# Low part of the first expert's down weights in each ring of four: made one unit later on VectorE, beside that of the second expert

## The chip, the cores and the metric

The kernel runs on one core of a Trainium2 chip. The metric is device time in microseconds (us) of one execution; lower is better. All positions in the trace are us from the start of the profiled span.

## The reference

One perceiver layer on x of shape (2, 128, 256), in float32: cross attention to 2048 context tokens (16 query heads, 8 key heads), causal self attention, and then the part in which the change lies, a mixture of experts:

```
shared = silu(x @ shared_gate_w) * (x @ shared_up_w) @ shared_down_w
comb   = weights of the 2 best of 16 experts for each token
for e in range(16):
    g, u = split(x @ experts_gate_up[e])
    routed = routed + comb[:, e:e+1] * (silu(g) * u @ experts_down[e])
out = x + shared + routed
```

Each expert has gate and up weights of 256 x 256 and down weights of 128 x 256. There are 256 token rows.

## The kernel before

Matrix products are made from float32 data split in two: a "high" part (the value rounded to the TensorE format fp32r) and a "low" part (value minus high part). Each product is three matmuls: low with high, high with low, high with high (lines 586 to 588). So every weight needs a rounding and a subtraction before TensorE may use it.

The expert stage handles 17 experts, numbered m = 0 to 16; m = 0 is the shared one, m = 1 to 16 are the routed ones. Weights live in rings of four slots (slot s = m % 4), and the loops step over rings: m = 4 i + s. Every engine has its own queue of instructions in program order, and they meet at semaphores:

- SyncE (SP) loads weights. For expert m it waits until the gate-up low part of m - 4 is made (`gu_ready`), issues the gate-up load (line 418), waits until the down low part of m - 4 is made (`dn_ready`), and issues the down load (line 420). Experts 0 to 7 are loaded long before the stage; 8 to 16 are loaded inside it.
- ScalarE (ACT), in its unit m: `silu` of the gate half (line 1528), then `round_gu`, the rounding of the gate-up weights of m + 3 (line 1542), which waits for their load; then the rounding of the gated rows (line 1559), then `round_dn`, the rounding of the down weights of m + 1 (line 1548).
- GpSimd (POOL): the low part of the gate-up weights, once they are rounded (line 455, from line 550). It begins with expert 4, when the router on VectorE is through.
- VectorE (DVE), in its unit m: `gated`, gate times up (line 2009); `add_expert` of m - 3, two instructions that add the product of an earlier expert to the rows (line 2047; line 2058 for the shared one); `rest_h`, the low part of the gated rows (line 2014); and the low part of the down weights of m + 1 (line 2066).
- TensorE (PE): `gate_up(m)`, 12 matmuls, then `down(m - 2)`, 6 matmuls. gate_up(m) waits for gate-up weights and for `gated` of m - 2. down(m) waits for the low parts of its weights and rows, and in the loop for `added3`, which comes with `add_expert(m - 2)`, that is with the additions of VectorE's unit m + 1:

```
pe.wait_ge(dn_ready, m + 1)
pe.wait_ge(h_lo_ready, m + 1)
after(pe, added3, B * (m - (RING if isinstance(m, int) else 2) + 1))
```

The loads on SyncE, in the order in which they are issued:

```
sp.wait_ge(gu_ready, m - RING + 1)
sp.dma_start(ring_gu[:, s], exgu_v[m - 1]).then_inc(ld_gu[s], 16)
sp.wait_ge(dn_ready, m - RING + 1)
sp.dma_start(ring_dn[:, s, :], ex_down_w[m - 1]).then_inc(ld_dn[s], 16)
```

In ScalarE's unit:

```
round_gu(m + 3, t, ...)     # waits for ld_gu[t]
act.wait_ge(h_ready, m + 1)
act.activation(hT_hi[:, s], hT[:, s % 2], ACT.Copy).then_inc(h_hi_ready, 1)
```

Of the kernel before, what the change touches and what calls it, by code (L numbers as in the profile page):

```python
# [5 lines left out]
ALU = mybir.AluOpType  # L6
ACT = mybir.ActivationFunctionType
AX = mybir.AxisListType
F32 = mybir.dt.float32
# [21 lines left out]
def perceiver_layer(nc, x, ctx_tokens, key_mask, xq_w, xk_w, xv_w, xo_w, sq_w, skv_w, sd_w,  # L31
                    gate_w, expert_bias, sh_gate_w, sh_up_w, sh_down_w, ex_gu_w, ex_down_w, out):
    B, T, H = x.shape
    _, KEYS, VIS = ctx_tokens.shape
    assert B == 2 and T == P and VIS == P and H == 2 * P
    HB = H // P
# [10 lines left out]
    E = gate_w.shape[1]  # L47
    F = ex_down_w.shape[1]
    RING = 4
# [30 lines left out]
    with ExitStack() as stack:  # L80
# [3 lines left out]
        def sem(name):  # L84
            return stack.enter_context(nc.semaphore(name))
# [17 lines left out]
        with nc.sbuf_tensor("first_pT", [P, J, NBLK, P], F32) as first:  # L103
# [63 lines left out]
            for v in (ctx_hi, ctx_lo))  # L167
        dn_hi, dn_lo = (v[:].rearrange("p b i d -> p (b i d)")[:, RING * HB * 2 * F:][:, 0:RING * H]
                        .rearrange("p (s n) -> p s n", s=RING) for v in (ctx_hi, ctx_lo))
# [12 lines left out]
        ring_dn = ctx_raw[:, 2048:3072].rearrange("p (s n) -> p s n", s=RING)  # L182
# [34 lines left out]
        def turned_block(f, s):  # L217
# [56 lines left out]
        dn_hi_ready, dn_ready, h_hi_ready, h_lo_ready = (  # L274
            sem("dn_hi_ready"), sem("dn_ready"), sem("h_hi_ready"), sem("h_lo_ready"))
# [306 lines left out]
        def _(pe):  # L582
# [336 lines left out]
            def query(r, head, cols, done):  # L919

                dst, h = (QA, QB)[head // 2], head % 2
                _, hi, lo = wq2_of[r % 2]
                for k in range(HB):
                    at = (k * HR + head) * P
                    last = product(dst[:, h * B * T + cols.start:h * B * T + cols.stop],
                                   (hi[:, at:at + P], lo[:, at:at + P]),
                                   [v[:, cols] for v in XT[k]], k == 0, k == HB - 1)
                if h == 1:
                    last.then_inc(done, 1)
# [644 lines left out]
        def _(dve):  # L1574
# [432 lines left out]
            def gated(m, s):  # L2007
                dve.wait_ge(silu_ready, m + 1)
                dve.tensor_tensor(hT[:, s % 2], GU[s % 2][:, B * T:2 * B * T], sg[:, s % 2],
                                  ALU.mult).then_inc(h_ready, 1)  # L2010

            def rest_h(m, s):
                dve.wait_ge(h_hi_ready, m + 1)
                dve.tensor_tensor(hT_lo[:, s], hT[:, s % 2], hT_hi[:, s].bitcast(F32),
                                  ALU.subtract).then_inc(h_lo_ready, 1)
# [27 lines left out]
            def add_expert(m, s):  # L2043
                dve.wait_ge(down_psum, m + 1)
                for b in range(B):
                    dve.wait_ge(added3, B * (m - 1) + b + 1)
                    dve.scalar_tensor_tensor(resid[:, b, :], DWN[s][:, b * H:(b + 1) * H],  # L2047
                                             comb[:, b, bass.ds(m - 1, 1)], resid[:, b, :],
                                             ALU.mult, ALU.add).then_inc(added3, 1)

            def unit(i, s, dn_on):
                m = RING * i + s
                gated(m, s)
                if isinstance(m, int) and m == RING - 1:

                    dve.wait_ge(down_psum, 1)
                    rows = resid[:].rearrange("p b n -> p (b n)")
                    dve.tensor_tensor(rows, DWN[0][:], rows, ALU.add).then_inc(added3, B)
                elif not isinstance(m, int) or m >= RING:
                    add_expert(m - 3, (s - 3) % RING)  # L2060
                rest_h(m, s)
                if dn_on:

                    dve.wait_ge(dn_hi_ready, m + 2)
                    t = (s + 1) % RING
                    dve.tensor_tensor(dn_lo[:, t], ring_dn[:, t], dn_hi[:, t].bitcast(F32),
                                      ALU.subtract).then_inc(dn_ready, 1)

            router()

            dve.wait_ge(dn_ready, RING)
            for s in range(2, RING):
                unit(0, s, s == RING - 1)
            with dve.Fori(1, E // RING - 1) as i:
                for s in range(RING):
                    unit(i, s, True)
            for s in range(RING):
                unit(E // RING - 1, s, s < RING - 1)
            add_expert(E - 3, 1)
            gated(E, 0)  # L2080
            add_expert(E - 2, 2)
# [35 lines left out]
```

## Time and profile before

| | |
|---|---|
| median of 3 runs | 344.44 us (343.89 to 344.46) |
| profiled execution, its time | 343.99 us |
| its span, first to last instruction | 342.2 us |
| mean granted TensorE clock | 0.993 |
| expert stage | from about 299 us to 340 us |

The span is what the trace shows; the execution's time lies 1.8 us above it. In rows of the timeline the columns are start and length in us, engine, line, operation, output <- inputs, shapes, count, and in brackets the idle time before with what ended it. In this part of the kernel `ctx_raw` holds the weights as loaded, the gated rows and the silu; `ctx_hi` and `ctx_lo` hold the high and low parts of the weights; `pT_hi` and `pT` hold those of the gated rows; `pair` and `bank` are PSUM banks.

### The profile page before, as it was taken

To read this page: it belongs to the slowest core of one execution; us is meant where nothing else is said; L and a number is where in the kernel's file an instruction comes from. 1 tells how busy PE (TensorE), PEld (TensorE's weight loads), DVE (VectorE), ACT (ScalarE), POOL (GpSimd) and SP (SyncE) were. 2 spreads that over 40 slices of the span, in tenths; PEclk is the share of its full clock that TensorE was granted. 3 is DMA by queue.
4 is the path that set the end of the run, shared out by engine and by line. 5 is a ranking of instruction groups with operands and counts; after the bars stand their busy time and mean duration, and the time that the engine had idled before them with its cause. 6 is when DMAs were issued, how large, how long until landed. Compare 5 with 4: busy or idle time off the path is not lost.

```text
span 342.2 us, 6811 instructions
## 1 busy us (share of the span) xinstructions
PE 329.7 (96%) x2222; PEld 299.0 (87%) x2222; DVE 270.4 (79%) x466; ACT 229.2 (67%) x410; POOL 220.2 (64%) x136
## 2 busy tenths in 40 slices
PE   6999988999999999999999999999999999899995
PEld 5887867999999999999999989899898897699995
DVE  2776888898988989889889889676558736479997
ACT  3799449586688777777777675993256666267761
POOL 3766709799499599499588786853625873117550
PEclk9999999999999999999999999999999999989999
DMA  6811558875896895885875976995052045004530
GB/s 211 244 33 38 115 134 192 218 167 132 219 211 140 205 206 124 213 200 124 200 183 115 206 176 175 204 268 178 2 164 84 0 156 153 3 0 131 178 107 32
DMA packets 32565, 49.98 MB, mean 146 GB/s; under 512 B 5536, under 2 KB 23072, under 8 KB 32544
## 3 DMA queue, kind: packets, MB, share of 16 engines
q1 hardware_dynamic: 32544, 49.72, 57.4%
q8 instruction: 11, 0.18, 0.2%
q14 instruction: 10, 0.08, 0.1%
HBM read 20.08 MB, written 0.26 MB: 59 GB/s over the span
## 4 chain that ended last, share of the span: by engine, by line
PE 86%; DVE 6%; ACT 4%; issue 2%; POOL 1%; DVEq 0%; POOLq 0%; ACTq 0%
PE bank L586 12%; PE bank L587 12%; PE bank L588 12%; PE pair L586 11%; PE pair L588 11%; PE pair L587 11%; PE bank L984 2%; PE bank L790 2%; PE bank L1014 1%; ACT probs L1253 1%; PE pair L977 1%; PE bank L977 1%; ACT first_pT L1334 1%; PE pair L943 1%; DVE resid L2047 1%
## 5 line engine op out<-in xcount | busy, mean ns | idle before, releaser
L455 POOL TENSOR_TENSOR pT<-pT,pT_hi 128x1024 fp32r<-128x1024 f32 x54 | 129.3, 2418 | 34.5 <-ACT pT_hi L1263 34.4
L1253 ACT ACTIVATE probs<-probs,lowest 128x2048 f32<-128x2048 f32 x32 | 64.4, 2012 | 23.3 <-DVE lowest L1650 23.3
L1263 ACT ACTIVATE pT_hi<-pT 128x1024 fp32r<-128x1024 f32 x56 | 57.7, 1055 | 12.7 <-DMA pT<-ctx_raw 11.6
L587 PE MATMUL bank<-pT,ctx_hi 128*128 128x256 f32 x224 | 64.2, 287 | 0.0
L586 PE MATMUL bank<-pT_hi,ctx_lo 128*128 128x256 f32 x224 | 63.9, 285 | 0.0
L588 PE MATMUL bank<-pT_hi,ctx_hi 128*128 128x256 f32 x224 | 63.6, 284 | 0.0
L586 PE MATMUL pair<-ctxT_hi,qk_lo 128*128 128x512 f32 x128 | 52.2, 408 | 0.0
L588 PE MATMUL pair<-ctxT_hi,qk_hi 128*128 128x512 f32 x128 | 50.1, 391 | 0.0
L587 PE MATMUL pair<-ctxT_lo,qk_hi 128*128 128x512 f32 x128 | 50.0, 391 | 0.0
L1650 DVE CUSTOM_DVE_ANT_0 probs<-pair,mask_bias,lowest 128x1024 f32<-128x1024 f32 x32 | 40.9, 1280 | 10.2 <-PE pair L588 9.5
L455 POOL TENSOR_TENSOR ctx_lo<-ctx_raw,ctx_hi 128x512 fp32r<-128x512 f32 (+1 forms) x19 | 31.4, 1666 | 23.8 <-ACT ctx_hi L1542 17.5
L1650 DVE CUSTOM_DVE_ANT_0 probs<-pair,mask_bias 128x1024 f32<-128x1024 f32 x32 | 38.5, 1205 | 6.7 <-PE pair L588 3.8
L586 PEld LDWEIGHTS bank<-pT_hi,ctx_lo 128*128 128x128 f32 x224 | 42.3, 189 | 1.7 <-POOL pT L455 0.8
L587 PEld LDWEIGHTS bank<-pT,ctx_hi 128*128 128x128 f32 x224 | 42.1, 188 | 1.0
L588 PEld LDWEIGHTS bank<-pT_hi,ctx_hi 128*128 128x128 f32 x224 | 42.7, 191 | 0.0
L1661 DVE STREAM_TRANSPOSE ctx_raw<-probs 128x2048 f32<-128x2048 f32 x14 | 32.0, 2308 | 0.5 <-PE bank L790 0.5
L1661 DVE STREAM_TRANSPOSE blocks<-probs 128x2048 f32<-128x2048 f32 x14 | 31.9, 2306 | 0.0
L588 PEld LDWEIGHTS pair<-ctxT_hi,qk_hi 128*128 128x128 f32 x128 | 24.0, 188 | 5.4
L586 PEld LDWEIGHTS pair<-ctxT_hi,qk_lo 128*128 128x128 f32 x128 | 24.1, 188 | 3.2
L587 PEld LDWEIGHTS pair<-ctxT_lo,qk_hi 128*128 128x128 f32 x128 | 24.2, 189 | 3.1
L586 PE MATMUL pair<-xnT_hi,ctx_lo 128*128 128x256 f32 x64 | 18.4, 288 | 0.0
L587 PE MATMUL pair<-xnT_lo,ctx_hi 128*128 128x256 f32 x64 | 18.4, 288 | 0.0
(280 smaller groups left out, 794.3 us busy)
## 6 DMA issues: line engine op xcount, KB each, us to landing
pT<-blocks SPq DMA_DIRECT2D x112, 128.0 KB, 2.3
pT<-ctx_raw SPq DMA_DIRECT2D x112, 128.0 KB, 2.3
ctx_raw<-ffn_experts_gate_up_dram SPq DMA_DIRECT2D x16, 256.0 KB, 2.9
wq<-in_L_xattn_Wq_dram SPq DMA_DIRECT2D x8, 256.0 KB, 2.7
ctx_raw<-in_ctx_dram SPq DMA_DIRECT2D x8, 256.0 KB, 6.5
wo<-in_L_xattn_Wo_dram SPq DMA_DIRECT2D x8, 256.0 KB, 3.0
blocks<-in_L_attn_w_dense_dram SPq DMA_DIRECT2D x4, 512.0 KB, 4.8
ctx_raw<-_L_ffn_experts_down_dram SPq DMA_DIRECT2D x16, 128.0 KB, 2.4
```

The source lines that it names most:

```text
L455: pool.tensor_tensor(dst, src, hi.bitcast(F32), ALU.subtract).then_inc(ready, 1)
L586: pe.matmul(dst, w[1], x[0], start=start, stop=False)
L587: pe.matmul(dst, w[0], x[1], start=False, stop=False)
L588: return pe.matmul(dst, w[0], x[0], start=False, stop=stop)
L790: last = pe.matmul(dst, ctx_raw[:, blk * P:(blk + 1) * P], first_pT[:, :, blk, :], start=(blk == 0), stop=(blk == NBLK - 1))
L943: last = pe.matmul(KV[:, (B + b) * P:(B + b + 1) * P], xnT[:, k, b * T:(b + 1) * T], wv2[:, k], start=(k == 0), stop=(k == HB - 1))
L977: mm = pe.matmul(SC[b][:, h * P:(h + 1) * P], q2T[:, h, b * T:(b + 1) * T], k2T[:, b * T:(b + 1) * T], start=True, stop=True)
L984: pe.matmul(PC[b][:], v2[:, b], p2T[:, b], start=True, stop=True).then_inc(c2_psum, 1)
L1253: act.activation(probs[:, j], probs[:, j], ACT.Exp, bias=lowest[:, p, j, 1:2], scale=-1.0, accum_out=den[:, p, j:j + 1]).then_inc(exps, 1)
L1263: act.activation(hi_slot(c), chunk(p, c).bitcast(F32), ACT.Copy).then_inc(pT_hi_ready, 1)
L1650: dve.tensor_tensor_reduce(out=probs[:, j, keys], in0=pair[m % 2][:], in1=mask_bias[:, p, keys], scale=-SCALE, scalar=lowest[:, p, j, 0:1] ...
L1661: dve.transpose(blocks[p][:, :, j].rearrange("p q k t -> p k q t"), probs[:, j].rearrange("p (k q t) -> p k q t", q=QD, t=LN)).then_inc(tu ...
```

## The change

VectorE's unit (i, s) now makes the low part of the down weights of expert 4 i (slot 0) in unit s = 0 of the same ring, behind `rest_h`, and right behind it that of expert 4 i + 1; units s = 1 and 2 make that of m + 1 as before; unit s = 3 makes none. Before, slot 0 of the next ring was made in unit s = 3. The number of instructions is the same (12), and each waits for its own rounding.

```
+            def rest_dn(m, t):
+                dve.wait_ge(dn_hi_ready, m + 1)
+                dve.tensor_tensor(dn_lo[:, t], ring_dn[:, t], dn_hi[:, t].bitcast(F32),
+                                  ALU.subtract).then_inc(dn_ready, 1)
+
...
                 rest_h(m, s)
-                if dn_on:
-
-                    dve.wait_ge(dn_hi_ready, m + 2)
-                    t = (s + 1) % RING
-                    dve.tensor_tensor(dn_lo[:, t], ring_dn[:, t], dn_hi[:, t].bitcast(F32),
-                                      ALU.subtract).then_inc(dn_ready, 1)
+                if dn_on and s == 0:
+                    rest_dn(m, 0)
+                if dn_on and s < RING - 1:
+                    rest_dn(m + 1, s + 1)
 
             router()
 
             dve.wait_ge(dn_ready, RING)
             for s in range(2, RING):
-                unit(0, s, s == RING - 1)
+                unit(0, s, False)
             with dve.Fori(1, E // RING - 1) as i:
                 for s in range(RING):
                     unit(i, s, True)
             for s in range(RING):
-                unit(E // RING - 1, s, s < RING - 1)
+                unit(E // RING - 1, s, True)
```

## Rows read from the trace of the kernel before

**Rows 1.** The page, busy time of each engine and its share of the span.

```profile
PE 329.7 (96%) x2222; PEld 299.0 (87%) x2222; DVE 270.4 (79%) x466; ACT 229.2 (67%) x410; POOL 220.2 (64%) x136
```

**Rows 2.** Busy time by stretch, for 6 us inside the expert stage.

```profile
318.00:324.00 6.00, 6.00 (x52) 5.95 (x51) 6.00 (x15) 4.61 (x12) 3.66 (x3) 1.00 0.56 172
```

**Rows 3.** Timeline of PE: last matmul before down(3), its first, down(6)'s, down(10)'s.

```profile
311.56 0.28 PE L588 MATMUL pair<-xnT_hi,ctx_hi 128*128 128x256 f32 x1
312.23 0.39 PE L586 MATMUL bank<-ctx_hi,pT 128*128 128x256 f32 x1 [0.40 <-DVE resid L2047]
...
318.73 0.39 PE L586 MATMUL bank<-ctx_hi,pT 128*128 128x256 f32 x1
...
327.46 0.29 PE L586 MATMUL bank<-ctx_hi,pT 128*128 128x256 f32 x1
```

**Rows 4.** Timeline of DVE: end of unit 3, units 4 and 5; rest_h(7); gated(15).

```profile
309.53 1.52 DVE L2066 TENSOR_TENSOR ctx_lo<-ctx_raw,ctx_hi 128x256 fp32r<-128x256 f32 x1
310.98 0.41 DVE L2009 TENSOR_TENSOR ctx_raw<-pair,ctx_raw 128x256 f32<-128x256 f32 x1
311.31 0.86 DVE L2047 SCALAR_TENSOR_TENSOR resid<-bank,route,resid 128x256 f32<-128x256 f32 x2
312.10 0.41 DVE L2014 TENSOR_TENSOR pT<-ctx_raw,pT_hi 128x256 fp32r<-128x256 f32 x1
...
312.77 0.41 DVE L2009 TENSOR_TENSOR ctx_raw<-pair,ctx_raw 128x256 f32<-128x256 f32 x1
...
318.60 0.76 DVE L2014 TENSOR_TENSOR pT<-ctx_raw,pT_hi 128x256 fp32r<-128x256 f32 x1
...
334.70 0.42 DVE L2009 TENSOR_TENSOR ctx_raw<-pair,ctx_raw 128x256 f32<-128x256 f32 x1 [0.16 <-ACT ctx_raw L1528]
```

**Rows 5.** Timeline of POOL: gate-up low parts of experts 4 to 7, then of 10.

```profile
306.60 5.60 POOL L455 TENSOR_TENSOR ctx_lo<-ctx_raw,ctx_hi 128x512 fp32r<-128x512 f32 x4 [9.20 <-ACT ctx_hi L1542]
...
317.77 1.30 POOL L455 TENSOR_TENSOR ctx_lo<-ctx_raw,ctx_hi 128x512 fp32r<-128x512 f32 x1 [0.83 <-ACT ctx_hi L1542]
```

**Rows 6.** Waits of SP's queue: us in total, times, longest.

```profile
SPq L420 <- DVE ctx_lo L2066: 10.9, 9, 2.6
```

**Rows 7.** Timeline of SP: down 8 and gate-up 9, down 12 and gate-up 13.

```profile
311.21 0.35 SPq L420 DMA_DIRECT2D ctx_raw<-_L_ffn_experts_down_dram  x1
311.81 0.37 SPq L418 DMA_DIRECT2D ctx_raw<-ffn_experts_gate_up_dram  x1
...
319.85 0.34 SPq L420 DMA_DIRECT2D ctx_raw<-_L_ffn_experts_down_dram  x1
320.44 0.37 SPq L418 DMA_DIRECT2D ctx_raw<-ffn_experts_gate_up_dram  x1
```

**Rows 8.** From issue to landing, us: gate-up load 9; all nine; down loads too.

```profile
ctx_raw<-ffn_experts_gate_up_dram SPq DMA_DIRECT2D x1, 256.0 KB, 3.0
...
ctx_raw<-ffn_experts_gate_up_dram SPq DMA_DIRECT2D x9, 256.0 KB, 2.8
...
DMA to landing us min/median/max: 2.0/2.6/3.2
```

**Rows 9.** Timeline of ACT: silu(4), round_gu(9), round_gu(13), silu(15).

```profile
309.74 0.38 ACT L1528 ACTIVATE ctx_raw<-pair 128x256 f32<-128x256 f32 x1 [0.47 <-PE pair L588]
...
314.94 0.62 ACT L1542 ACTIVATE ctx_hi<-ctx_raw 128x512 fp32r<-128x512 f32 x1
...
323.58 0.62 ACT L1542 ACTIVATE ctx_hi<-ctx_raw 128x512 fp32r<-128x512 f32 x1
...
334.28 0.39 ACT L1528 ACTIVATE ctx_raw<-pair 128x256 f32<-128x256 f32 x1 [0.43 <-PE pair L588]
```

**Rows 10.** Busy time by stretch around the router: after PE, PEld, DVE, ACT, POOL, the granted clock.

```profile
297.00:298.00 1.00, 0.16 (x1) 0.14 (x1) 0.56 (x3) 0.00 (x1) 0.40 (x1) 1.00 0.00 0
...
300.00:301.00 1.00, 1.00 (x7) 1.00 (x6) 0.90 (x4) 1.00 (x1) 0.00 (x0) 0.50 0.00 0
...
303.00:304.00 1.00, 1.00 (x9) 1.00 (x8) 0.83 (x6) 0.18 (x2) 0.00 (x0) 0.82 0.00 0
```

## The prediction

> **What bounds the kernel now.** I read the page first: PE is busy 96% of the span [rows 1]. The change touches only the expert stage, so I then took the table by stretch there. In 6 us of it PE and DVE are both busy all the time, ACT 4.61 us, POOL 3.66 us, at full clock [rows 2]. Two engines at 100% call for the timelines, to see which waits for which. A unit on PE takes 2.13 us: 18 matmuls, about 0.118 us apart; 12 of gate_up take 1.42, 6 of down 0.71. PE really waits at one place: the last matmul of gate_up(5) starts at 311.56, so down(3) could start at 311.68, and it starts at 312.23, released by the additions on DVE (line 2047) [rows 3]. Those end at 311.31 + 0.86 = 312.17 [rows 4], so additions to PE takes 0.06. Its first matmul has 0.39 where others have 0.28: the load of its weights is no longer hidden behind matmuls, 0.1 more. down(6) shows the same 0.39 at 318.73, while down(10) at 327.46 has 0.29 [rows 3]. So PE sets the pace and DVE's additions come just in time, with 0 to 0.2 to spare.
>
> DVE's own work in a unit is less than 2.13: starts lie 0.33 apart for gated, 0.79 for two additions, 0.33 for rest_h, 0.33 for the down subtraction, 1.78 in all. The rest is a blockage. POOL works from 317.77 to 319.07 [rows 5]; rest_h(7) starts at 318.60 and takes 0.76 instead of 0.41 [rows 4], ending at 319.36, 0.29 behind POOL. The down subtraction in unit 3 takes 1.52 us and ends at 311.05, 0.25 behind the third of POOL's four in a row, of 1.4 each [rows 4, 5]. That instruction is the one that the change moves out, and it is what made down(3) late.
>
> Last, the waits of SP's queue: nine times line 420 waits for DVE line 2066, 10.9 us in total [rows 6]. Each down load waits for the very subtraction that is moved, and the gate-up load of the next expert stands behind it in the same queue.
>
> **The change, part by part.** It adds no work: 12 subtractions stay 12. Four effects follow.
>
> *Unit 3 loses its subtraction (gain).* Where DVE is free, gated starts 0.42 behind silu: 334.28 and 334.70 [rows 4, 9]. So gated(4) can start at 309.74 + 0.42 = 310.16, not 310.98. The additions end 0.33 + 0.86 later, at 311.35. down(3) starts at 311.68: 0.55 + 0.1 = 0.65 gained.
>
> *Unit 4 has two subtractions (loss).* rest_h(4) still ends behind POOL's fourth, which ends 306.60 + 5.60 = 312.20 [rows 5], perhaps 0.13 earlier as DVE no longer disturbs it: 312.35. Subtractions end at 312.68 (expert 4) and 313.01 (expert 5), gated(5) follows, and the additions end at 314.13. PE reaches down(4) at 311.68 + 0.71 + 1.42 = 313.81 and starts at 314.19 + 0.1, where before it started at 314.46. So 0.65 shrinks to about 0.2 within one unit. In the later rings the second subtraction alone would make the additions 0.33 later where they have 0.16 to spare: 0.17 + 0.06 + 0.1, some 0.3 a ring.
>
> *The loads.* Before, the subtraction of expert 4 ended at 311.05, down load 8 was issued at 311.21 and gate-up load 9 at 311.81, 0.60 behind [rows 4, 7]. Now it ends at 312.68, so down 8 goes out at 312.84 and gate-up 9 at 313.44. Its landing took 3.0, the nine have a median of 2.8 [rows 8]; I take 2.9: 316.35. Before, it landed at 314.81 and ACT used it at 314.94 [rows 9]: 0.13 to spare against 1.63 of delay. gate_up(6) now ends at 312.39 + 1.42 + 0.16 = 313.97, silu(6) follows at 314.12, and 0.28 later, at 314.40, ACT wants the load. It stands for 1.95.
>
> *What is queued behind that wait.* round_gu(9) then ends at 316.35 + 0.62 = 316.97. Behind it on ACT stands the rounding of gated rows 6, done at about 317.4; POOL starts 0.08 behind round_gu, at 317.05, and holds DVE's rest_h(6) until 318.35 + 0.28 = 318.63. The subtraction starts at 318.55, gated(7) at 318.88, the additions at 319.21, ending at 320.07. down(6), which needs them, starts at 320.13 instead of 318.73: **+1.4**. The gain of 0.2 is inside this number.
>
> Of these 1.4, POOL's hold on DVE is a good half: were rest_h(6) free at 317.4, it would end at 317.8 and down(6) would start near 319.3, +0.6. The Trainium skill's page SBUF — State Buffer, section "Who interferes with whom", says that a VectorE instruction with two SBUF inputs and a GpSimd instruction that reads SBUF exclude each other, and that whoever issued first keeps the port for its whole instruction. By that rule it is +1.4, and the 0.76 of [rows 4] agrees; without it, it would be +0.6.
>
> *The second ring.* PE now runs 1.4 late, so DVE and ACT have caught up with it, and the double subtraction costs nothing there: the rounding of gated rows 7, held up by gated(7), lets ACT come to silu(8) at 320.05 and round_gu(11) at 320.33, POOL's low part of 11 runs from 321.03 to 322.33, rest_h(8) ends at 322.61, the subtraction of expert 8 at 322.94. down 12 goes out at 323.10, gate-up 13 at 323.70 (before 320.44 [rows 7]), landing 2.8 later, 326.5. gate_up(10) ends at 324.66 (before 323.26), and ACT wants to round at 324.98 (before 323.58 [rows 9]). It stands for 1.5. The same chain follows: round 0.62, POOL to 328.5, rest_h(10) to 328.78, subtraction, gated, additions to 330.23, down(10) at 330.3 instead of 327.46 [rows 3]: **+2.8** in all.
>
> *The third ring.* There is no gate-up load 17, and down load 16 (out at about 333 now) lands 2 us later, with the last product wanted at 340. Gate-up 16 lands by 332.6, wanted at 333.0: 0.4 to spare. Small waits of PE such as that at 318.73, here some 0.1 in all, vanish as DVE now has slack. The tail is tied to PE and moves with it.
>
> Sum: 1.4 + 1.4 - 0.1 = +2.7. On the profiled execution's 343.99 that is 346.7; the median of the runs lies 0.45 above that execution, so 347.1 on it. I say 347.0.
>
> Bounds: all loads of the stage, the half as large down loads too, landed within 2.0 to 3.2 [rows 8], so each wait may be up to 0.8 shorter or 0.3 longer: +1.1 to +3.3. The gate-up loads are nearest to their own median of 2.8. Not shown in the trace is how ACT behaves when it waits for a load in this stage; from below it costs nothing beyond the landing, as I take it, from above 0.1 each.
> The Trainium skill's page DMA: Bandwidth & Descriptors, section "Anatomy of one DMA", fits a load as 2.0 us plus bytes over 436 GB/s (for loads issued by GpSimd); for 256 KB that is an estimate of 2.6 us. With it the sum would be about +2.2; the measured 2.8 to 3.0 decide.
>
> **The rivals.**
> *One stall only.* The delay that the first wait gives PE might serve the second ring as slack: if DVE, far ahead, gets rest_h(8) in before POOL's instruction at 321.03, expert 8's low part is done 1.6 earlier and gate-up 13 comes in time. For it: ACT starts silu(8) at once after the hold-up, and DVE adds are over at about 321.6, only 0.6 behind POOL's start. Against: 0.6 is more than what any small shift gives. +1.3: 345.3 to 345.8. Chance 0.10.
> *The clock falls.* Before, the granted clock was 1.00 while PE was busy 0.16 of a us at 297, and it stood at 0.50, the lower of its two levels (1.2 GHz), from 300 until within the us from 303 [rows 10], with PE busy throughout. The new waits leave PE idle for about 1.5 each. A low spell of some 3.2 us at half the clock does 1.6 us of full-clock work, so it loses 1.6. Behind the first wait it would be mostly absorbed by the second (PE wants gate-up 13 later too); behind the second it is paid: 2.7 + 1.6 = +4.3, 348.3 to 348.7. Against: both waits lie between dense stretches, and the shorter wait at 312 has full clock behind it [rows 2]. Chance 0.10.
> The Trainium skill's page TensorE: Matmul & The Clock Gate, section "The HAM clock gate", says that the low clock is the idle state and that sustained activity lifts it, which leaves this open.
> *The loads are hidden anyway*, because ACT's wait falls in time that nobody needs. Then the first ring gives 0.2, the others lose 0.3 each: +0.1 to +0.4, 344.1 to 344.8. Against: only 0.13 to spare [rows 8, 9]. Chance 0.06.
> *Faster.* The moved subtraction frees unit 3 from POOL's four in a row, and the 0.65 at down(3) stays gained, with the waits at down(6) and its like, 0.35 in all: -1.0, 343.0 to 343.4. It decides if rest_h(4) and both subtractions end before 312.0, so before POOL's fourth. That one starts at about 310.8, and rest_h(4) can't before 311.35. Chance 0.04.
>
> **How the numbers follow.** Forecast 0.70, with its own range of 345.9 to 347.7 (each wait 0.3 off, on either base). One stall 0.10, clock 0.10, hidden 0.06, faster 0.04. 345.3 to 348.7 leaves out hidden and faster, 1 in 10. A measurement of this kernel can tell 0.2%, 0.7 us, from no change: faster is 0.04, within is 0.07 (the hidden case and a little of the one-stall case), slower is 0.89.
>
> **What would show it.** In the profile of the changed kernel: down(3) starts without the 0.40 of idle time; gate-up load 9 is issued near 313.4 and 13 near 323.7; ACT line 1542 waits twice for a DMA, 1.5 to 2 us each; POOL and then rest_h (line 2014) follow, over 1 us long each time; PE waits twice for DVE line 2047, at down(6) and down(10), about 1.5 each; the third ring runs without waits. I am wrong if line 1542 has no wait for DMA, if PE's waits lie elsewhere, or if the clock is at 0.50 after them.

## The result and the profile after

The changed kernel takes 347.19 us (median of 4 runs, 347.02 to 347.58) against 344.29 us: ratio 1.0087, interval 1.0075 to 1.0100, so 2.9 us slower. The forecast was 347.0 with a range of 345.3 to 348.7. The profiled execution took 347.58 us, its span is 345.8 us, the mean granted clock 0.993 as before.

The table by stretch, for the same 6 us as [rows 2] (the columns are PE, PEld, DVE, ACT, POOL, then the clock). PE was busy all of them before; now it has 4.53:

```profile
318.00:324.00 6.00, 4.53 (x39) 4.33 (x38) 6.00 (x14) 4.09 (x11) 3.36 (x4) 1.00 0.41 116
```

The waits from 303 us on (us in total, times, longest):

```profile
ACT ctx_hi L1542 <- DMA ctx_raw<-ffn_experts_gate_up_dram: 4.2, 4, 2.0
...
PE bank L586 <- DVE resid L2047: 2.7, 2, 1.5
...
PE pair L586 <- DVE resid L2047: 0.2, 1, 0.2
```

The first line is new: ScalarE's rounding of gate-up weights waits for the loads, four times. PE waits for the additions twice in earnest. The timeline of PE, first matmuls of down(3), down(4), down(6) and down(10), to be held against [rows 3]:

```profile
312.07 0.28 PE L586 MATMUL bank<-ctx_hi,pT 128*128 128x256 f32 x1
...
314.55 0.39 PE L586 MATMUL pair<-ctx_hi,pT 128*128 128x256 f32 x1 [0.18 <-DVE resid L2047]
...
320.54 0.39 PE L586 MATMUL bank<-ctx_hi,pT 128*128 128x256 f32 x1 [1.47 <-DVE resid L2047]
...
330.62 0.39 PE L586 MATMUL bank<-ctx_hi,pT 128*128 128x256 f32 x1 [1.19 <-DVE resid L2047]
```

The wait at down(3) is gone, a smaller one has come at down(4), and then two long ones. Upstream of them, SP's queue (against [rows 7]), with down 8 and gate-up 9, down 12 and gate-up 13:

```profile
313.19 0.35 SPq L420 DMA_DIRECT2D ctx_raw<-_L_ffn_experts_down_dram  x1
313.79 0.37 SPq L418 DMA_DIRECT2D ctx_raw<-ffn_experts_gate_up_dram  x1
...
323.40 0.35 SPq L420 DMA_DIRECT2D ctx_raw<-_L_ffn_experts_down_dram  x1
324.00 0.37 SPq L418 DMA_DIRECT2D ctx_raw<-ffn_experts_gate_up_dram  x1
```

ACT's round_gu(9), round_gu(10) and round_gu(13) (against [rows 9]), each with the wait for its load:

```profile
316.75 0.63 ACT L1542 ACTIVATE ctx_hi<-ctx_raw 128x512 fp32r<-128x512 f32 x1 [1.97 <-DMA ctx_raw<-ffn_experts_gate_up_dram]
...
318.87 0.63 ACT L1542 ACTIVATE ctx_hi<-ctx_raw 128x512 fp32r<-128x512 f32 x1 [0.61 <-DMA ctx_raw<-ffn_experts_gate_up_dram]
...
326.84 0.63 ACT L1542 ACTIVATE ctx_hi<-ctx_raw 128x512 fp32r<-128x512 f32 x1 [1.35 <-DMA ctx_raw<-ffn_experts_gate_up_dram]
```

Loads 9 and 13 landed 2.9 and 2.8 us behind their issue. Load 10 stood in a row of six loads that SP issued 0.54 to 0.60 apart from 313.19 on; it went out at 314.89 and took 3.9 us, where before it took 3.2. ACT's waits for loads 10 and 14 are short (0.61 and 0.23 us), ACT waits for `gated` behind each of them anyway (0.23 and 0.60 us), and PE doesn't wait for them.

POOL follows each long wait, and holds DVE (against [rows 5, 4]). First POOL's gate-up low parts of 9 and 13:

```profile
317.46 1.29 POOL L455 TENSOR_TENSOR ctx_lo<-ctx_raw,ctx_hi 128x512 fp32r<-128x512 f32 x1 [2.91 <-ACT ctx_hi L1542]
...
327.55 1.29 POOL L455 TENSOR_TENSOR ctx_lo<-ctx_raw,ctx_hi 128x512 fp32r<-128x512 f32 x1 [2.30 <-ACT ctx_hi L1542]
```

Then DVE: gated(4), rest_h(4), the two subtractions of unit 4, and rest_h(6):

```profile
310.56 0.42 DVE L2009 TENSOR_TENSOR ctx_raw<-pair,ctx_raw 128x256 f32<-128x256 f32 x1 [0.56 <-ACT ctx_raw L1528]
...
311.70 1.00 DVE L2014 TENSOR_TENSOR pT<-ctx_raw,pT_hi 128x256 fp32r<-128x256 f32 x1
312.62 0.75 DVE L2053 TENSOR_TENSOR ctx_lo<-ctx_raw,ctx_hi 128x256 fp32r<-128x256 f32 x2
...
317.72 1.31 DVE L2014 TENSOR_TENSOR pT<-ctx_raw,pT_hi 128x256 fp32r<-128x256 f32 x1 [1.44 <-ACT pT_hi L1559]
```

rest_h(6) starts at 317.72, POOL has been at work since 317.46 and ends at 318.75, and rest_h(6) ends at 319.03, 0.28 behind it, for 1.31 us instead of 0.41. The third ring has no wait of PE over 0.1.

All of this lies in a profile that enters the stage 0.40 us later than the one before: down(2) starts at 309.94 instead of 309.54. To compare executions I use **the stage**: from the first matmul of down(2) to the first of down(14). Before it is 336.17 - 309.54 = 26.63, after it is 339.41 - 309.94 = 29.47: +2.84. The profiled executions differ by 3.59: 0.40 ahead of the stage, 2.84 in it, 0.23 given back between down(14) and the last addition, and 0.6 more from the last addition to the end of the output stores.

### The profile page after: what moved, and what is told of

It reads as the page before. It is cut to its first block, busy times and chain, and to the rows that moved or that the text cites. A ratio compares the mean times of both kernels' runs of the same rounds, so it can differ in the third digit from the quotient of the medians.

```text
span 345.8 us, 6809 instructions
## 1 busy us (share of the span) xinstructions
PE 330.2 (95%) x2222; PEld 298.8 (86%) x2222; DVE 270.6 (78%) x466; ACT 228.9 (66%) x410; POOL 220.0 (64%) x136
## 4 chain that ended last, share of the span: by engine, by line
PE 71%; DVE 12%; issue 5%; ACT 5%; DMA 3%; POOL 2%; SPq 0%; DVEq 0%; POOLq 0%; ACTq 0%
PE bank L586 11%; PE bank L587 10%; PE bank L588 10%; PE pair L586 8%; PE pair L587 8%; PE pair L588 8%; DVE probs L1650 3%; PE bank L984 2%; PE bank L790 2%; DVE resid L2047 2%; ACT probs L1253 2%; DMA ctx_raw<-ffn_experts_gate_up_dram 2%; DVE pT L2014 1%; PE bank L1014 1%; PE pair L977 1%
## 5 line engine op out<-in xcount | busy, mean ns | idle before, releaser
L586 PE MATMUL bank<-pT_hi,ctx_lo 128*128 128x256 f32 x224 | 63.9, 285 | 0.0
L588 PE MATMUL bank<-pT_hi,ctx_hi 128*128 128x256 f32 x224 | 63.5, 284 | 0.0
L586 PE MATMUL pair<-ctxT_hi,qk_lo 128*128 128x512 f32 x128 | 52.2, 408 | 0.0
L588 PE MATMUL pair<-ctxT_hi,qk_hi 128*128 128x512 f32 x128 | 50.1, 391 | 0.0
L586 PEld LDWEIGHTS bank<-pT_hi,ctx_lo 128*128 128x128 f32 x224 | 42.3, 189 | 1.9 <-POOL pT L455 0.9
L588 PEld LDWEIGHTS bank<-pT_hi,ctx_hi 128*128 128x128 f32 x224 | 42.7, 191 | 0.0
L588 PEld LDWEIGHTS pair<-ctxT_hi,qk_hi 128*128 128x128 f32 x128 | 24.0, 188 | 5.4
L586 PEld LDWEIGHTS pair<-ctxT_hi,qk_lo 128*128 128x128 f32 x128 | 24.1, 188 | 3.2
L586 PE MATMUL pair<-xnT_hi,ctx_lo 128*128 128x256 f32 x64 | 18.3, 287 | 0.0
L1680 DVE SCALAR_TENSOR_TENSOR resid<-bank,rden,resid 128x256 f32<-128x256 f32 x32 | 15.4, 481 | 3.8 <-PE bank L588 3.2
```

What stands on the lines that cost most here:

```text
L586: pe.matmul(dst, w[1], x[0], start=start, stop=False)
L588: return pe.matmul(dst, w[0], x[0], start=False, stop=stop)
L1680: dve.scalar_tensor_tensor(resid[:, b, :], YO_BANK[:, j * H:(j + 1) * H], rden[:, p, j:j + 1], resid[:, b, :], ALU.mult, ALU.add).then_inc ...
```

## The experiments

Each ratio is to the kernel before, run on the same chip. It is not always the ratio of the two medians (e9 and e10 differ by 2.6 us in their medians and by 2.1 in their ratios). The stage comes from the trace of one execution. That execution is not always a typical one: e4's is the fastest of its four, e10's the fastest of four, e9's the slowest of ten. Edits shift the line numbers: L588 and L2049 in the rows of e1 and e9 are L586 and L2047 of the changed kernel.

| run | what differs | median, us | ratio (95%) | stage, us |
|---|---|---|---|---|
| before | | 344.07 to 344.32 | 1 | 26.63 |
| changed | | 347.19 | 1.0087 (1.0075 to 1.0100) | 29.47 |
| e1 | changed, gate-up loads first | 344.74 | 1.0019 (1.0005 to 1.0032) | 27.05 |
| e2 | before, gate-up loads first | 344.29 | 0.9996 (0.9987 to 1.0005) | 26.59 |
| e3 | before, loads late | 348.16 | 1.0115 (1.0100 to 1.0130) | 31.17 |
| e4 | moved for expert 4 alone | 346.24 | 1.0063 (1.0045 to 1.0080) | 27.93 |
| e12 | moved for expert 8 alone | 346.12 | 1.0055 (1.0039 to 1.0072) | 28.62 |
| e8 | before, DVE's loop written out | 344.05 | 0.9997 (0.9984 to 1.0010) | 26.60 |
| e5 | changed, looser wait of down | 347.51 | 1.0093 (1.0079 to 1.0107) | 28.39 |
| e6 | before, looser wait of down | 344.35 | 1.0012 (0.9994 to 1.0031) | 25.60 |
| e7 | changed, both | 344.79 | 1.0014 (0.9998 to 1.0031) | 25.60 |
| e11 | before, both | 343.71 | 0.9984 (0.9972 to 0.9995) | 25.60 |
| e9 | changed, short POOL work | 345.04 | 1.0018 (1.0008 to 1.0028) | 27.82 |
| e10 | before, short POOL work | 342.45 | 0.9956 (0.9938 to 0.9973) | 25.60 |

25.60 is 12 units of 2.133: PE without any wait.

**Is it the loads?** e1 and e2 change only SyncE's order:

```
-                sp.wait_ge(gu_ready, m - RING + 1)
-                sp.dma_start(ring_gu[:, s], exgu_v[m - 1]).then_inc(ld_gu[s], 16)
-                sp.wait_ge(dn_ready, m - RING + 1)
-                sp.dma_start(ring_dn[:, s, :], ex_down_w[m - 1]).then_inc(ld_dn[s], 16)
+            load_gu(RING, 0)
+            with sp.Fori(1, E // RING) as i:
+                for s in range(RING):
+                    load_gu(RING * i + s + 1, (s + 1) % RING)
+                    load_dn(RING * i + s, s)
+            load_dn(E, 0)
```

> The changed kernel, but SyncE issues the gate-up load of m + 1 ahead of the down load of m, so that it no longer stands behind the wait for the moved subtraction. Theory (late loads behind that wait): ScalarE's waits for gate-up loads 9 and 13 are gone, and with them TensorE's two waits of 1.5 and 1.2 us; the first ring keeps a gain of 0.2, the double subtraction costs up to 0.3 in each of the two later rings: 344.1 to 344.8. Rival (the double subtraction itself makes TensorE late): 346.5 to 347.2, TensorE's waits stay.

> The kernel before with the same order of the loads as in the run above, and nothing else. Theory: gate-up load 9 had 0.13 us to spare and no engine waited for a load, so an earlier load gives nothing: within 0.2% of before, 343.9 to 344.6. Rival (loads already cost something before the change, in a way that no wait shows): over 0.7 us faster.

e1: 344.74, no wait of ACT for a load; of the 2.9 us 0.6 are left. PE's waits for the additions in e1's trace:

```profile
PE pair L588 <- DVE resid L2049: 0.7, 3, 0.3
```

Three waits, at down(4), down(8) and down(12), of 0.18, 0.26 and 0.24 us, each with 0.1 more in its first matmul. The idle time in brackets begins only where the last matmul's overlapping 0.28 us end; counted from start to start, each wait delays the next unit by 0.44 to 0.52 us. The kernel before has small waits of its own, so I compare whole rings of e1 with it: -0.21 in the first (down(2) to down(6)), +0.32 in the second, +0.31 in the third. That is the cost of the double subtraction once the loads are out of the way. e2: nothing. So the order of the loads costs nothing by itself; it costs because the moved subtraction stands ahead of a load in it.

e3 makes the loads late and leaves DVE alone:

```
-                sp.wait_ge(dn_ready, m - RING + 1)
+                sp.wait_ge(dn_ready, m - RING + (2 if s == 0 else 1))
```

> The kernel before, VectorE untouched, but for slot 0 SyncE waits for one low part more before it issues the down load, so gate-up loads 9 and 13 go out about 2 us later while the subtraction stays where it was. Theory: load 9 is issued near 313.6 and lands near 316.5, ScalarE waits 1.5 us for it and again about 1.5 for load 13, TensorE waits at down(6) and down(10), sum +2.8 to +3.0: 347.0 to 347.4. Rival (double subtraction): no change, 344.3.

The direction is as expected, the size is not: +3.9 (4.54 in the stage) instead of +2.8 to +3.0. The two expected waits are there, and a third that was not. e3's timeline of PE, down(6), down(7), down(10):

```profile
319.93 0.39 PE L586 MATMUL bank<-ctx_hi,pT 128*128 128x256 f32 x1 [1.59 <-DVE resid L2047]
...
323.50 0.39 PE L586 MATMUL bank<-ctx_hi,pT 128*128 128x256 f32 x1 [1.18 <-DVE resid L2047]
...
331.40 0.38 PE L586 MATMUL bank<-ctx_hi,pT 128*128 128x256 f32 x1 [1.26 <-DVE resid L2047]
```

The third wait comes from load 10. It was issued at 314.09 and took 4.5 us, ACT waited for it as well, and so handed the roundings of 10 and 11 to POOL close together. POOL works 2.7 us in a row, and both of DVE's subtractions of unit 7 are held. ACT's round_gu(10), then POOL, then DVE:

```profile
318.63 0.63 ACT L1542 ACTIVATE ctx_hi<-ctx_raw 128x512 fp32r<-128x512 f32 x1 [0.97 <-DMA ctx_raw<-ffn_experts_gate_up_dram]
```

```profile
319.33 2.71 POOL L455 TENSOR_TENSOR ctx_lo<-ctx_raw,ctx_hi 128x512 fp32r<-128x512 f32 x2 [1.19 <-ACT ctx_hi L1542]
```

```profile
319.80 1.10 DVE L2014 TENSOR_TENSOR pT<-ctx_raw,pT_hi 128x256 fp32r<-128x256 f32 x1
320.82 1.50 DVE L2066 TENSOR_TENSOR ctx_lo<-ctx_raw,ctx_hi 128x256 fp32r<-128x256 f32 x1
```

The 1.50 us instruction is the subtraction of expert 8. In the changed kernel unit 7 has none, and down(7) doesn't wait. So late loads alone cost more than the whole change does, by 1.0 us in the medians and 1.70 in the stage. That the empty unit s = 3 gives this back is my reading and is not shown: load 10 also landed later in e3 (4.5 us behind its issue against 3.9), and no run separates the two.

**Are the two waits two effects?** e4 and e12 move one expert's subtraction each. DVE's loop over rings 1 and 2 is written out for that; e8 is the control. The core of e4, and of e12:

```
+                if dn_on and i == 1 and s == 0:
+                    rest_dn(m, 0)
+                if dn_on and (s < RING - 1 or i < E // RING - 1):
+                    rest_dn(m + 1, (s + 1) % RING)
...
+                if dn_on and i == 2 and s == 0:
+                    rest_dn(m, 0)
+                if dn_on and (s < RING - 1 or i in (0, 2)):
+                    rest_dn(m + 1, (s + 1) % RING)
```

> The changed kernel, but only expert 4 (ring 1) has its subtraction moved; experts 8 and 12 have theirs in unit s = 3 as before (VectorE's loop over two rings is written out for it). Theory: one wait for a load (9), one wait of TensorE, at down(6), and load 13 in time: half of the loss, +1.3 to +1.5, 345.5 to 345.9. Rival (each double subtraction costs about a third of the loss, three of them in all): +1.0, 345.3, without a wait of ScalarE for load 9.

> The kernel before with VectorE's loop over two rings written out and nothing else: the control for the run that moved the subtraction in ring 1 only, whose median lay 0.9 above what the waits in its trace account for. If writing out costs, this run is 0.5 to 0.9 slower than before; if that was scatter, within 0.5 of before.

> Only expert 8 (ring 2) has its subtraction moved; experts 4 and 12 have theirs in unit s = 3 as before (VectorE's loop written out, which alone cost nothing). Theory: load 9 in time, load 13 late, ScalarE waits for it about 1.8 us, and here the double subtraction isn't hidden, so down(8) waits as well, 0.2 to 0.3; TensorE's down(10) comes 1.6 to 1.8 later. In the trace, from down(2) to down(14), 28.2 to 28.5 us against 26.6 of before and 29.5 of the changed kernel; time 345.8 to 346.1. Rival (the second stall of the changed kernel is a consequence of the first): 344.3 to 344.6, no wait of ScalarE for load 13.

e8: within 0.1% of before. e4 has one wait for load 9 (1.76 us) with one of PE behind it (1.26 us), another of ACT for load 10 (0.77 us), load 13 in time, and its stage is 1.30 longer, as expected; its median lies 0.3 above the expected range, with runs from 344.46 to 346.96. Writing the loop out is not the reason (e8); the excess stays open. e12 has load 9 in time and load 13 late. Its timeline of ACT, round_gu(13):

```profile
325.86 0.63 ACT L1542 ACTIVATE ctx_hi<-ctx_raw 128x512 fp32r<-128x512 f32 x1 [1.89 <-DMA ctx_raw<-ffn_experts_gate_up_dram]
```

Its stage is 1.99 longer, 28.62 where 28.2 to 28.5 was expected; its time is +2.0 by the medians, 346.12, at the upper end of what was expected. Each wait comes without the other, so the two effects are separate. Their sum, 1.30 + 1.99 = 3.29, is more than the 2.84 of both together. e12's down(8), 0.2 late with 0.1 more in its first matmul, shows the double subtraction; in the changed kernel down(8) follows down(7) by 2.13 us, without a delay, so there it is hidden behind the first wait.

**Does the early wait of down matter?** down(m) waits for the additions of m - 2, though its bank is free with those of m - 4. e5, e6, e7 and e11 relax that:

```
-                after(pe, added3, B * (m - (RING if isinstance(m, int) else 2) + 1))
+                after(pe, added3, B * (m - RING + 1))
...
-            with pe.Fori(1, E // RING) as i:
+            def ring(i):
...
+            ring(1)
+            with pe.Fori(2, E // RING) as i:
+                ring(i)
```

> The changed kernel, but TensorE's down(m) waits only for the additions of m - 4, which free its bank, not for those of m - 2 (its first ring is written out for it). Theory: the loads of 9 and 13 stay late; down(6) then waits for the low part of its rows alone, which comes when TensorE does, and down(10) waits some 1.4 us for it: half of the loss goes, 345.2 to 346.2. Rival (TensorE needs those additions in time for another reason, so that the wait only changes its place): no gain, 347.0 and more.

> The kernel before with the same looser wait. Theory: TensorE's 0.65 us at down(3) and the small waits behind it, about 1.0 in all, are gone, nothing else is near: 343.0 to 343.6. Rival (VectorE is the real bound of the stage): no change, 344.2, with the wait at another place.

> The changed kernel with both: gate-up loads ahead of the waiting down loads, and the looser wait of down. Theory: no wait of ScalarE for a load and none of TensorE in the stage, so the same time as the kernel before with the looser wait: 343.0 to 343.6. Rival (the double subtraction costs by itself): slower than that one by over 0.5.

> The kernel before with gate-up loads ahead of the waiting down loads and with the looser wait of down, the version that the runs so far point to. Theory A (the spread of 3 us of the two runs with the looser wait comes from loads that land just too late, ScalarE waited 1.7 us for them in one trace): with the loads earlier the runs keep to 343.0 to 343.8. Theory B (it comes from something behind the stage, such as the last store, whose issue took 1.4 us in that trace): the spread stays, 343.2 to 346, median 344.2 to 344.8.

e5 refutes its theory. PE's stage shrinks by 1.08 and the time doesn't: 347.51. The last addition on DVE, the changed kernel's and then e5's:

```profile
342.39 0.47 DVE L2089 SCALAR_TENSOR_TENSOR resid<-bank,route,resid 128x256 f32<-128x256 f32 x1
```

```profile
342.18 0.47 DVE L2093 SCALAR_TENSOR_TENSOR resid<-bank,route,resid 128x256 f32<-128x256 f32 x1
```

Counted from down(2), that is 32.45 and 32.34: the chain through loads, ACT, POOL and DVE ends where it did. PE comes earlier, and ACT waits for loads that much longer (6.2 us in all from 303 us on, 4.2 in the changed kernel). PE's waits are where the loss is seen, not where it is made.

e6, e7 and e11 all reach the 25.60 of a PE without waits. Their times do not follow: 343.0 to 343.6 was expected of e6 and e7, and their medians are 344.35 and 344.79. So taking away PE's waits of 1.0 us didn't by itself make the kernel faster. ACT waits for loads in both, five times in e6 (1.7 us in all) and once in e7 (0.6), where no such wait was expected. Only e11 is measurably faster than before, by 0.16%, less than the 0.2% that I count as told from no change. e6 ran from 343.16 to 346.53 us, e7 from 343.3 to 346.09, e11 from 342.51 to 344.71. In e6's trace the last addition starts 1.0 us earlier than before, counted from down(2), and one of the two output stores has an issue of 1.43 us (min, median, max of the two):

```profile
L430 SPq DMA_DIRECT2D out_dram<-resid x2: 361/893/1425, 338.1 to 338.6; - x2
```

e7's trace has the same 1.43, e11's, the changed kernel's and that of before have 0.34 to 0.43. That accounts for single executions; what spreads the others was not seen. e11 fits theory A in its median, but not in its spread. The question stays open.

**What does POOL's hold cost?** e9 and e10 make only 16 of 512 columns of the gate-up low parts from expert 4 on.

```
+                n = HB * 2 * F if isinstance(i, int) and i == 0 else 16
+                rest(gu_lo[:, s, 0:n], ring_gu[:, s].rearrange("p k f -> p (k f)")[:, 0:n], gu_hi[:, s, 0:n],
+                     gu_ready)
```

> The changed kernel, with GpSimd making only 16 of the 512 columns of the gate-up low parts from expert 4 on (the other columns keep old values, so the products of these experts are not the reference's), so that it hardly holds VectorE. Theory: the loads of 9 and 13 are as late as in the changed kernel, ScalarE still waits about 2 and 1.5 us, but rest_h(6) and rest_h(10) no longer wait for GpSimd; TensorE waits some 0.6 at down(6) and at down(10) instead of 1.5 and 1.2. Against the kernel before with the same short GpSimd work: +1.2 to +1.5, where the change alone gave +2.9. Rival (GpSimd's hold plays no part in the loss): TensorE's waits stay at 1.5 and 1.2, and the difference stays near +2.9.

> The kernel before with the same short GpSimd work (16 of 512 columns of the gate-up low parts from expert 4 on, so not the reference's products): the control for the run above. Theory: no hold on VectorE, so no wait at down(3) and no 0.39 at down(6), (9), (12): the stage about 1.0 shorter in its trace, 343.0 to 343.6. Rival (GpSimd's hold is hidden): 344.2.

e10 is 1.9 us faster than before by the medians (1.5 by the ratio), more than expected; its stage is at the floor, 1.03 shorter, and the rest lies outside it. e9's timeline of PE, down(6) and down(10):

```profile
319.81 0.39 PE L588 MATMUL bank<-ctx_hi,pT 128*128 128x256 f32 x1 [0.45 <-DVE resid L2049]
...
329.85 0.39 PE L588 MATMUL bank<-ctx_hi,pT 128*128 128x256 f32 x1 [0.93 <-DVE resid L2049]
```

From down(2) to down(6) e9 takes 9.14, its control 8.53: +0.61, where the changed kernel has 10.60 against 9.19, +1.41. That is the half foretold for the first wait, though two other differences nearly cancel in it: counted from down(2), load 9 comes 0.57 earlier in e9 than in the changed kernel, and down(6) 0.66 earlier in the control than before. The hold itself is read from the start of round_gu(9) to the next additions: 2.87 us in the changed kernel (316.75 to 319.62), 1.98 in e9 (316.91 to 318.89), so 0.89.

But e9 and e10 differ by 2.22 in the stage and 0.62% in time, 2.1 us, not by 1.2 to 1.5, and ACT waits 1.38 and 1.87 for loads 9 and 13, not 2 and 1.5. In the second ring nothing is won: down(6) to down(10) takes 10.04 in e9 and 10.08 in the changed kernel. Counted from down(2), ACT wants load 13 at 14.41 in e9 and at 15.55 in the changed kernel, and gets it at 16.28 and 16.90. Without the hold PE is 1.14 earlier and the load only 0.62, so it is waited for longer (1.87 us against 1.35). Besides, e9's load 10 took 4.3 us, and down(7) comes 0.2 later for it. So POOL's hold makes the first wait longer, and taking it away doesn't shorten the second ring.

## Why the prediction was right

Positions of the profile after, less the 0.40 us by which it enters the stage later, against the predicted ones:

| step | predicted | found |
|---|---|---|
| down(3) starts | 311.68 | 311.67 |
| gate-up load 9 issued | 313.44 | 313.39 |
| round_gu(9) starts | 316.35 | 316.35 |
| rest_h(6) ends | 318.63 | 318.63 |
| down(6) starts | 320.13 | 320.14 |
| gate-up load 13 issued | 323.70 | 323.60 |
| round_gu(13) starts | 326.5 | 326.44 |
| down(10) starts | 330.3 | 330.22 |

- **The gain of unit 3** came, 0.65 at down(3), and was mostly lost at down(4). That starts 0.31 earlier than before (314.55 - 0.40 against 314.46), with 0.1 more in its first matmul: 0.2 is left, as foretold, and down(5) starts 0.21 earlier (316.78 - 0.40 against 316.59).
- **The late load** is the cause. Shown from both sides: without it (e1) 0.6 us are left, and with it alone (e3) all of the loss and more is there. The waits for loads 10 and 14 were not foretold; they cost nothing here.
- **What is queued behind it**: round_gu, POOL, rest_h, additions, down, in that order. POOL's share of the first wait was put at 1.4 - 0.6 = 0.8; read directly it is 0.89 (e9). What I did not say is that the sum doesn't shrink by that share.
- **The double subtraction** was put at 0.3 a ring where nothing hides it, and is 0.32 and 0.31 in the second and third ring of e1 against before. That the second ring hides it is borne out by e12: with no first wait ahead of it, down(8) comes 0.2 late.
- **The small waits** were to vanish in the third ring, 0.1, "as DVE now has slack". They didn't all: down(13) still has 0.39, and so has down(9). DVE has no slack there: it is busy in every us from 328 to 342, and e5, with less waiting of PE, ends only 0.1 earlier. By ring the change costs 1.41, 1.35 and 0.08, against 1.4, 1.4 and -0.1: the stage is +2.84 instead of +2.7.
- **What was luck.** The two load times were taken as 2.9 and 2.8 us and came so; other gate-up loads of the same trace took up to 3.9, beyond the 2.0 to 3.2 from which the bounds were made, and up to 4.5 in e3. The forecast of 347.0 rests on a median of 344.44 for the kernel before, which is 344.29 in the runs made beside the changed kernel; this 0.15 too much covers the 0.14 too little in the sum.
- **Slips in the working.** Each wait 0.3 off, on either base, gives 346.1 to 347.7, not 345.9 to 347.7. The low spell in [rows 10] adds up to about 3.4 us rather than 3.2, so the rival of the clock would have cost 1.7. Neither changes the forecast.
- **The rivals.** One stall only: no, there are two, and each comes without the other. The loads hidden: no. Faster: no, the three instructions could not end before 312.0; rest_h(4) alone ended at 312.30 (312.70 less the 0.40). The clock: no. Every us from 316 to the end has it at 1.00. Below, the changed kernel in the two waits, where PE was busy for 0.07, 0.44 and 0.38 of a us, with the clock at 1.00:

```profile
319.00:320.00 1.00, 0.07 (x1) 0.00 (x0) 1.00 (x4) 0.77 (x2) 0.42 (x1) 1.00 0.09 31
...
329.00:330.00 1.00, 0.44 (x4) 0.23 (x3) 1.00 (x4) 0.40 (x2) 0.70 (x1) 1.00 0.02 6
330.00:331.00 1.00, 0.38 (x3) 0.38 (x4) 1.00 (x4) 1.00 (x4) 0.58 (x1) 1.00 0.28 49
```

## What to carry to other kernels

Before moving an instruction, list who waits for its semaphore, and then what stands behind each waiter in its own queue: here the waiter was a down load that had time, and the gate-up load behind it had 0.13 us. A queue that waits for two kinds of buffers in turn should issue the kind with the least time to spare first (e1; before the change the same order gained nothing, e2). The engine at which a loss is seen may only be its last stop: e5 took 1 us of PE's waits away and the end did not move.

## What the runs showed of the hardware that I had not expected

A spell of half clock ahead of the stage is in nine of the fourteen traces and not in the other five, though the instructions ahead of the stage are the same. From 300 to 302 us e4 ran at 1.00, the changed kernel at 0.50, both after a wait of 1.07 us for the normalised rows (`xn`) at 297 to 298. e4's row comes first, then the changed kernel's:

```profile
300.00:302.00 2.00, 2.00 (x19) 2.00 (x19) 1.75 (x8) 1.45 (x2) 0.00 (x0) 1.00 0.00 0
```

```profile
300.00:302.00 2.00, 2.00 (x11) 2.00 (x11) 1.65 (x8) 1.25 (x1) 0.00 (x0) 0.50 0.00 0
```

The traces with full clock there enter the stage at 308.2 to 309.3, those with the spell at 309.5 to 310.7. In time it shows less: of the executions of the kernel before beside e1, the five with a mean clock of at most 0.996 have a median 0.35 us above that of the seventeen with at least 0.999; beside e5 it is nine and eighteen, and 0.02 us. The scatter has nothing to do with the change, and is one reason to compare the stage and not only the end.
